# Local attention of a two-layer transformer: float32r projections in three parts, the row maximum given to the exponential as a bias, another order of the slot

## The reference, cut to what matters

```python
h = shift_token(x)                       # upper half of the features comes from the token before
q, k, v = jnp.split(h @ wqkv, 3, axis=-1)          # wqkv: 128 x 1536, f32; 8 heads of 64
q = l2norm(q) * qs;  k = l2norm(k) * ksc
q, k = rotary_xpos(q, k)                 # x * cos * scale + rotate_half(x) * sin * scale
sim = jnp.einsum('bhwid,bhwjd->bhwij', q * 8, look_around(k))   # windows of 64, own and one before
attn = jax.nn.softmax(jnp.where(mask, -finfo.max, sim), axis=-1)
x = x + (attn @ look_around(v)) @ wo
h = layernorm(shift_token(x)) ...;  x = x + (a * gelu(g)) @ w2 + b2     # feed-forward, hidden 341
```

## Time and profile before

| | |
|---|---|
| timed runs, median (lowest to highest) | 1535.98 us (1535.06 to 1538.76), 3 runs |
| the profiled execution's own time / its span | 1539.69 us / 1537.8 us |
| PE busy | 1338.7 us, 87% of the span |
| DVE busy | 1145.2 us, 74% |
| ACT busy | 799.3 us, 52% |
| POOL busy | 724.0 us, 47% |
| granted TensorE clock, mean | 0.946 of full speed |
| chain that ended last | POOL 24% (L1537 14%, L1530 11%), DVE 8%, SP's queue 7% |

### The profile page before, as it was taken

How to read it: one execution, slowest core, us unless ns; L and a number is a source line. 1 busy time by engine, 2 the same in 40 slices (tenths; PEclk the granted TensorE clock), 3 DMA queues, 4 the chain that set the end, 5 groups by cost and what they waited for, 6 DMA issues and landing times.

```text
span 1537.8 us, 39029 instructions
## 1 busy us (share of the span) xinstructions
PE 1338.7 (87%) x15968; PEld 966.2 (63%) x15968; DVE 1145.2 (74%) x2484; ACT 799.3 (52%) x1633; POOL 724.0 (47%) x562
## 2 busy tenths in 40 slices
PE   4545999987999999994799999977889999999787
PEld 3434888875777777772466666654556666666554
DVE  4776766534888888873799999974569999999465
ACT  1222223223666666663677777743347777776321
POOL 1752455442333443334666666632146666666100
PEclk7876899996999999997999999999999999999999
DMA  4000555410000000002000100011100000000011
GB/s 135 0 0 7 111 106 112 89 30 5 3 3 3 3 3 3 3 4 89 10 9 8 22 9 9 1 30 27 24 25 10 9 14 17 9 5 5 10 37 48
DMA packets 61837, 40.34 MB, mean 26 GB/s; under 512 B 41312, under 2 KB 51808, under 8 KB 61664
## 3 DMA queue, kind: packets, MB, share of 16 engines
q1 hardware_dynamic: 61664, 37.88, 10.5%
HBM read 27.12 MB, written 2.36 MB: 19 GB/s over the span
## 4 chain that ended last, share of the span: by engine, by line
POOL 24%; DVE 8%; SPq 7%; issue 7%; PE 4%; ACT 2%; DMA 1%; DVEq 0%; POOLq 0%; ACTq 0%
POOL rot L1537 14%; POOL rn L1530 11%; SPq L1463 6%; DVE qk L1631 5%; DVE e_pm L1614 1%; PE PS L2018 1%; PE PS L2027 1%; PE PS L1962 1%; DVE e_mx L1610 1%; PE PS L1877 0%; SPq L1460 0%; SPq L1459 0%; DMA qks<-in_e_ks 0%; PE PS L1919 0%; DVE xn L1682 0%
## 5 line engine op out<-in xcount | busy, mean ns | idle before, releaser
L1537 POOL TENSOR_TENSOR rot<-qk,sinl 128x1024 f32<-128x1024 f32 x64 | 217.7, 3401 | 112.1 <-DVE qk L1631 112.1
L1530 POOL TENSOR_TENSOR rn<-ss,neghalf 128x16 f32<-128x16 f32 x64 | 185.6, 2900 | 108.5 <-DVE ss L1624 108.5
L1102 DVE TENSOR_REDUCE d_mx<-PS 128x4 f32<-128x576 f32 x128 | 96.9, 757 | 66.3 <-PE PS L1246 63.3
L1877 PE MATMUL PS<-wqkv,hT 128*128 128x512 f32 x256 | 129.7, 630 | 7.4 <-DMA qks<-in_e_ks 5.5
L1757 ACT ACTIVATE qk<-PS 128x512 f32<-128x512 f32 x128 | 76.2, 597 | 104.3 <-PE PS L1877 104.3
L607 POOL TENSOR_TENSOR uu<-uu,cb 128x512 f32<-128x512 f32 x64 | 82.7, 1294 | 90.0 <-DVE uu L839 88.5
L739 ACT ACTIVATE sg<-PS 128x512 f32<-128x512 f32 x72 | 43.0, 597 | 134.2 <-PE PS L667 134.2
L1928 PEld LDWEIGHTS PS<-ident,e_pm 128*128 128x128 f32 x512 | 58.4, 141 | 80.1 <-issue 80.1
L1165 ACT ACTIVATE pa<-PS 128x512 f32<-128x512 f32 x128 | 76.5, 597 | 61.8 <-PE PS L1255 61.7
L839 DVE TENSOR_TENSOR uu<-sg,PS 128x512 f32<-128x512 f32 x72 | 49.4, 687 | 66.8 <-ACT sg L739 66.0
L1246 PE MATMUL PS<-kx,d_q 32*64 32x256 f32 (+1 forms) x2048 | 98.0, 306 | 0.0
(11 more groups left out here) (241 smaller groups left out, 3535.1 us busy)
## 6 DMA issues: line engine op xcount, KB each, us to landing
cb<-comb_rows SPq DMA_DIRECT2D x32, 512.0 KB, 9.1
X<-in_L_attn_x SPq DMA_DIRECT2D x4, 512.0 KB, 7.1
...
```

The lines of the kernel that those rows point to most:

```text
L1102: chain(dve.tensor_reduce(mx[:, par, :, :], s, AX.X, ALU.max))
L1530: pool.tensor_tensor(rn[:, v % 2, :], ss[:, v % 2, :], c.neghalf[:, :], ALU.pow).then_inc(rn_ready.sem, 1)
L1537: pool.tensor_tensor(rot[:, :, :, :], x, bc(sinl[:, t, :, :], 2, H2), ALU.mult).then_inc(rot_ready.sem, 1)
L1877: pe.matmul(PS[:, QBANK + s, :], h_of(v), wqkv[:, s * INNER:(s + 1) * INNER], start=True, stop=True).then_inc(eqkv_ready.sem, 1)
```

## The change

In `local_transformer`:

- The projections take float32r operands in two parts each. ACT rounds the weights to `w_hi` by thirds (`round_weights`), DVE (layer 0) or POOL (layer 1) makes `w_lo = w - w_hi`; ACT's copy of the turned features becomes `h_hi`, and a new DVE step `low` makes `h_lo`. Each projection is then three accumulating matmuls (`project`): hi by hi, hi by lo, lo by hi. k is projected before q.
- DVE no longer subtracts the maximum. It writes the negated maximum, and ACT's exponential reads the scores in PSUM with it as bias: eight activations of 128x128 in a unit in place of two of 128x512.
- The mask's matmuls (`hide`) are a step of their own in the slot before, and wait for all exponentials of the unit before.
- The turned features go into 128 unused columns of OBANK (of QBANK for the first five units of layer 1).
- Every engine's `attend` has a new order; `clamp` stands before `rotated`, `squares` moves one slot later, `turn_p(u, 0)` moves one slot earlier, `features(u+4)` stands first on ACT.
- SP's load of layer 1's weights no longer waits for layer 0's last v projection.

```diff
+        w_hi, w_lo = ssb("wqkv_hi", [P, 3 * INNER], F32R), ssb("wqkv_lo", [P, 3 * INNER], F32R)
+        h_hi, h_lo = ssb("e_h_hi", [P, 4, P], F32R), ssb("e_h_lo", [P, 4, P], F32R)
...
+        def turned_z(L, v):
+            return PS[:, QBANK, 3 * P:4 * P] if L and v < 5 else PS[:, OBANK, 3 * P:4 * P]
+
+        def third(k):
+            return slice(k * INNER, (k + 1) * INNER)
...
-                        sp.wait_ge(ev_psum.sem, ev_psum.at(nunits * L))
+                        sp.wait_ge(wlo_ready.sem, wlo_ready.at(3 * L))
...
+                def split_weights(L, k):
+                    pool.wait_ge(whi_ready.sem, whi_ready.at(3 * L + k + 1))
+                    pool.tensor_tensor(w_lo[:, third(k)], wqkv[:, third(k)], w_hi[:, third(k)], ALU.subtract).then_inc(wlo_ready.sem, 1)
...
+                            split_weights(L + 1, g)
...
-                def shift(L, v):
+                def low(L, v):
+                    dve.wait_ge(eh_ready.sem, eh_ready.at(n(L, v)))
+                    dve.tensor_tensor(h_lo[:, v % 4, :], turned_z(L, v), h_hi[:, v % 4, :], ALU.subtract).then_inc(el_ready.sem, 1)
+
+                def maxima(L, v):
                     dve.wait_ge(s_ready.sem, s_ready.at(n(L, v)))
+                    if n(L, v) > 2:
+                        dve.wait_ge(p_exp.sem, p_exp.at(2 * (n(L, v) - 2)))
                     s = PS[:, SBANK:SBANK + 2, :].rearrange("p r (j k) -> p r j k", k=2 * W2)
-                    steps(dve.tensor_reduce(mx[:, :, :], s, AX.X, ALU.max))
-                    for h in range(2):
-                        if n(L, v) > 2:
-                            dve.wait_ge(pT_psum.sem, pT_psum.at(2 * (n(L, v) - 2) - 1 + h))
-                        dve.tensor_tensor(pm[:, v % 2, h, :, :, :], s[:, :, 2 * h:2 * h + 2, :],
-                                          bc(mx[:, :, 2 * h:2 * h + 2], 3, 2 * W2), ALU.subtract).then_inc(p_shifted.sem, 1)
+                    dve.tensor_reduce(mx[:, v % 2, :, :], s, AX.X, ALU.max, negate=True).then_inc(max_ready.sem, 1)
...
+                    if has(u + 4) and (u >= 0 or L == 0):
+                        low(L, u + 4)
                     if has(u):
-                        shift(L, u)
+                        maxima(L, u)
                     if u == nunits - 3:
                         apply(L, 0)
                     if has(u + 2):
@@ -1656,12 +1670,11 @@
                         square_sums(L, u + 3)
                     if has(u - 1):
                         divide(L, u - 1, 0)
+                        divide(L, u - 1, 1)
+                    if has(u + 3):
+                        clamp(L, u + 3)
                     if has(u + 2):
                         rotated(L, u + 2)
-                    if has(u + 3):
-                        clamp(L, u + 3)
-                    if has(u - 1):
-                        divide(L, u - 1, 1)
...
+                        if L + 1 < DEPTH and lead(g) is not None:
+                            low(L + 1, lead(g) + 4)
...
-                    last.then_inc(qk_taken.sem, 1)
+                    act.activation(h_hi[:, v % 4, :], turned_z(L, v), ACT.Copy).then_inc(eh_ready.sem, 1)
+
+                def round_weights(L, k):
+                    if k == 0:
+                        act.wait_ge(qkv_loaded.sem, qkv_loaded.at(16 * 3 * (L + 1)))
+                        if L:
+                            act.wait_ge(ev_psum.sem, ev_psum.at(nunits * L))
+                    act.activation(w_hi[:, third(k)], wqkv[:, third(k)], ACT.Copy).then_inc(whi_ready.sem, 1)
+
+                def take_features(L, v, s):
+                    act.wait_ge(eqkv_ready.sem, eqkv_ready.at(2 * n(L, v) - s))
+                    act.activation(qk[:, v % 4, s, :, :].rearrange("p h e -> p (h e)"), PS[:, QBANK + s, :],
+                                   ACT.Copy).then_inc(qk_taken.sem, 1)
...
-                def exponent(L, v, h):
-                    act.wait_ge(p_shifted.sem, p_shifted.at(2 * n(L, v) - 1 + h))
-                    p = pm[:, v % 2, h, :, :, :].rearrange("p r j k -> p (r j k)")
-                    act.activation(p, p, ACT.Exp).then_inc(p_exp.sem, 1)
+                def exponent(L, v, h, r):
+                    if h == 0 and r == 0:
+                        act.wait_ge(max_ready.sem, max_ready.at(n(L, v)))
+                    if n(L, v) > 2 and r == 0:
+                        act.wait_ge(pT_psum.sem, pT_psum.at(2 * (n(L, v) - 2) - 1 + h))
+                    for j in range(2):
+                        at = 2 * h + j
+                        last = act.activation(pm[:, v % 2, h, r, j, :], PS[:, SBANK + r, at * KEYS2:(at + 1) * KEYS2], ACT.Exp,
+                                              bias=mx[:, v % 2, r, at:at + 1])
+                    if r == 1:
+                        last.then_inc(p_exp.sem, 1)
...
                 def attend(L, u):
-                    if has(u + 4):
-                        take_features(L, u + 4)
+                    if has(u + 4) and (u >= 0 or L == 0):
+                        features(L, u + 4)
                     if has(u - 1):
                         take_p(L, u - 1, 0)
+                    if has(u + 3):
+                        squares(L, u + 3)
+                    if u == nunits - 1:
+                        whole(L, 0)
+                    if has(u + 4):
+                        take_features(L, u + 4, 1)
                     if has(u):
-                        exponent(L, u, 0)
+                        exponent(L, u, 0, 0)
+                    if has(u + 4):
+                        take_features(L, u + 4, 0)
+                    if has(u - 1):
+                        take_p(L, u - 1, 1)
                     if has(u + 2):
                         values(L, u + 2)
-                    if u == nunits - 1:
-                        whole(L, 0)
-                    if has(u - 1):
-                        take_p(L, u - 1, 1)
                     if has(u):
-                        exponent(L, u, 1)
+                        exponent(L, u, 1, 0)
+                        exponent(L, u, 0, 1)
                     if has(u - 2):
                         take_o(L, u - 2)
+                    if has(u):
+                        exponent(L, u, 1, 1)
                     if has(u + 1):
                         take_qk(L, u + 1)
-                    if has(u + 5) and (u >= -1 or L == 0):
-                        features(L, u + 5)
-                    if has(u + 4):
-                        squares(L, u + 4)
...
+                        if L + 1 < DEPTH and g < 3:
+                            round_weights(L + 1, g)
...
                     t, b = tile(v)
-                    if has(v - 4):
+                    if has(v - 6):
+                        pe.wait_ge(o_ready.sem, o_ready.at(2 * n(L, v - 6) - 1))
+                    elif L and has(v - 4):
                         pe.wait_ge(qkT_ready.sem, qkT_ready.at(n(L, v - 4)))
-                    elif has(v - 1):
-                        pe.wait_ge(qk_taken.sem, qk_taken.at(n(L, v - 1)))
+                    elif L and has(v - 1):
+                        pe.wait_ge(qk_taken.sem, qk_taken.at(2 * n(L, v - 1)))
                     elif L:
                         pe.wait_ge(qkT_ready.sem, qkT_ready.at(nunits * L))
                         pe.wait_ge(fT_ready.sem, fT_ready.at(G * (L - 1) + 1))
                     pe.wait_ge(zs_loaded[b].sem, zs_loaded[b].at(48 * (TB * L + t + 1)))
-                    pe.transpose(PS[:, QBANK, 0:P], zs[:, b, :], ident[:, :]).then_inc(zsT_psum.sem, 1)
+                    pe.transpose(turned_z(L, v), zs[:, b, :], ident[:, :]).then_inc(zsT_psum.sem, 1)
+
+                def project(to, v, k):
+                    pe.matmul(to, h_hi[:, v % 4, :], w_hi[:, third(k)], start=True, stop=False)
+                    pe.matmul(to, h_hi[:, v % 4, :], w_lo[:, third(k)], start=False, stop=False)
+                    return pe.matmul(to, h_lo[:, v % 4, :], w_hi[:, third(k)], start=False, stop=True)
 
                 def project_qk(L, v):
-                    pe.wait_ge(eh_ready.sem, eh_ready.at(n(L, v)))
-                    if v == 0:
-                        pe.wait_ge(qkv_loaded.sem, qkv_loaded.at(16 * 3 * (L + 1)))
-                    for s in range(2):
-                        pe.matmul(PS[:, QBANK + s, :], h_of(v), wqkv[:, s * INNER:(s + 1) * INNER],
-                                  start=True, stop=True).then_inc(eqkv_ready.sem, 1)
+                    pe.wait_ge(el_ready.sem, el_ready.at(n(L, v)))
+                    if has(v - 4):
+                        pe.wait_ge(qkT_ready.sem, qkT_ready.at(n(L, v - 4)))
+                    elif has(v - 1):
+                        pe.wait_ge(qk_taken.sem, qk_taken.at(2 * n(L, v - 1)))
+                    for s in (1, 0):
+                        if v == 0:
+                            pe.wait_ge(wlo_ready.sem, wlo_ready.at(3 * L + s + 1))
+                        project(PS[:, QBANK + s, :], v, s).then_inc(eqkv_ready.sem, 1)
...
-                def scores(L, v):
```

(24 more changed lines are left out.)

39 lines of the change are left out of this document (21 added, 18 removed).

## The result

The changed kernel takes 1478.86 us (median; 1477.64 to 1480.76), the kernel before on the same chip 1535.52 (1534.95 to 1538.76): ratio 0.9625, 95% interval 0.9609 to 0.9640, 57 us less. The forecast was 1490, 46 less; the time lies at the low end of the range of 1478 to 1514. The profiled execution took 1477.64, its span 1475.9.

What follows compares the result with a forecast made beforehand. The DVE-POOL loop was taken to set the 9.34 us slot, PE close behind; a PE-bound slot of 8.65 saves 0.69 over 62 slots, 43 us, plus 3 at the edges: 46 off the 1535.98 median, 1490 us, range 1478 to 1514.

Steps and rivals of the forecast that it cites:

- what bounds the kernel: Local attention's old slot of 9.34 us: set by the DVE-POOL-DVE loop, with PE's pure work close behind at about 9.05.
- PE's order: PE's sequence in a slot: the new order closes both waits for ACT's copies, 0.30 us a slot.
- the start: Start of layer 0: low part behind DVE's tables delays the first norm some 4 us, 2 won back; cost 2.
- its two holes: PE's waits before the second turn of the probabilities and before the output projection, put at 0.15 us each.
- Split projections: PE's q, k, v projections: nine float32r instructions at 0.232 us, 2.21 instead of 2.67 a slot.
- Rival (c): PE's projections: float32r runs at the f32 instruction's 0.427 us, +1.0 a slot, 1595 us; chance 0.04.
- Biased exponentials: ACT: eight exponentials with bias at 0.255 us each, net +1.0 a slot, ACT from 6.9 to 7.9 us.
- The loop: DVE and POOL with the clamp before the sums: norm, sine, power and hand-overs fall to 7.7 us.
- The small waits: Head and end of PE's slot: low part and turned q/k arrive in time, with 0.1 to 0.5 us to spare.
- rival (b): PE's slot: low part and turned q/k late by 0.1 to 0.15 each, slot 8.85 to 8.95, about 1506 us; chance 0.16.
- Rival (a): ACT becomes the bound: biased exponentials don't overlap, 0.37 us each, slot about 9.1, 1518 us; chance 0.11.
- The edges: Starts and last slots of the layers: 5 us back in the last slots, 2 lost at the start, together -3.

Runs made afterwards that it cites:

- the run with the clamp late: The changed kernel with the clamp put back behind the rotation's sums on DVE: 1523.24 us, ratio 0.991 to the kernel before.
- the kernel with two products: The changed kernel without the product of the features' high part by the weights' low part, six float32r instructions a unit for nine: 1468.03 us, ratio 0.9558 to before.
- f32 in the new order: The changed kernel with each projection as one f32 matmul in place of three float32r, all other work kept: 1503.04 us, ratio 0.9786 to before.
- the run with 64 columns: The changed kernel with four of a unit's eight exponentials of 128 columns each cut into two of 64: 1500.77 us, ratio 0.9774 to before.
- the run that undoes it: The changed kernel with the first unit's low part made before DVE's tables instead of behind them: 1477.54 us, ratio 0.9625 to before.

## Why the prediction was right in its parts, wrong in what bounded the slot, and short in the size

The time came out 11 us below the forecast. Two steps failed. The sentence on what bounds the kernel was wrong, and cost nothing in the time; the term of PE's order was mis-sized, and with it the slot: 8.65 was taken and 8.49 was run. 62 slots at 0.16 are 10 of the 11 us. That the rest fits so well is luck: the start cost 5 more than was taken, and the two drains gave 4.6 that nobody forecast.

- **What bounds the kernel.** "This loop over two engines sets the slot. PE is close behind." is the step that failed. PE with its two holes set the slot (9.35); the loop stood 0.16 below, at 9.19 (the run with the clamp late). The rows I read, norm to norm 9.34, are the same for both: an interval in a steady pipeline is the slot whichever chain sets it. What tells them apart is the slack in a chain, and the earlier trace rows has it: neither norm has a wait beside it, so it follows the instruction before it on DVE and not the power. The power of 907.65 ends at 910.55 and the norm starts 0.25 later; in the kernel with two products, where the norm does wait for the power (five times in 50 us, 1.1 in all), it starts 0.09 after the power (892.09 + 3.32 = 895.41, norm 895.50). The 0.16 between the two is the slack that the run with the late clamp showed. The start of layer 0 in the trace of before had the answer as well: its first 17 sines come 9.17 to 9.23 apart, with the norm 0.09 to 0.14 after the power, while the scores are 9.34 to 9.38 apart from the fourth interval on. The loop ran ahead of PE until PE held it. Since the sum was made for both limits, this error cost nothing in the time.
- **Split projections.** 0.232 and 0.46 a slot: right (0.23 to 0.24; 0.46). Rival (c) is out. Within it v was 0.70 by forecast and holds PE for 0.88 (888.72 to 889.60), for it now stands between two other shapes; the turn before it is 0.08 shorter.
- **PE's order.** The term was mis-sized: 0.30 for the holes was taken, 0.40 was measured. By PE's rows, from start to start, before against f32 in the new order: the second hole 0.14 (the weighing ahead of it 0.76, now 0.62), the output projection, which no longer waits for its operand, 0.11, the mask 0.10, the turns of q, k and o 0.10, the v projection only 0.04 where its hole of 0.15 was to close, and two other rows 0.07 longer (each rounded, so the sum is off by 0.02). The 0.05 to 0.1 that I added, because my walk of the old order gave 9.25 for 9.34, was about this 0.1 with the wrong sign: 8.58 became 8.65 where 8.49 was run.
- **Biased exponentials.** 0.25 from start to start where 0.255 was taken. The Trainium skill (ScalarE: Activation LUTs, What ACT_TABLE_LOAD costs) gave 0.29 by estimate; the rows are 0.04 below it, so the measurement decides. For 64 columns the same estimate is 0.24, and 0.20 was run.
- **The loop.** 7.7 forecast, 8.28 run, in the first slots of a layer and with two products: the power waits for the running sum (+0.4) and starts behind sine and clamp (+0.17). In the kernel as changed the slack above it is 0.2, not 0.9.
- **The small waits.** Low part hidden by 0.33 (forecast 0.15), turned k by 0.44: rival (b) did not happen. Rival (a) did not either, but the run with 64 columns puts it some 0.3 us of ACT away.
- **The edges.** The last slots gave some 6 (forecast 5), and the drains 2.3 each, which was not forecast. The start cost 7.2 for 2. 5.3 of it lie ahead of the first projection. I counted the low part behind the tables, 3.4 by the run that undoes it, but called the roundings and splittings of the weights free: the first projection waited for the weights' load before (10.6 behind the memset) and with the low part first still starts 1.9 later. The other 1.9 come behind it: each further projection waits for its own copy and subtraction (0.97, 0.97 and 3.15), and those up to 731 run at 0.43 and not 0.23 an instruction, since the clock rises later than before.
